# Cross attention of a decoder layer on one Trainium2 core: where VectorE's routing steps stand in a round

## The reference

```python
x = layernorm(x + linear_attention(x))                 # 16 heads of 8
lat, src = layer_norm(x), layer_norm(ctx)              # cross attention, 16 heads of 64
q = lat @ Wq;  k, v = split(concat([src, lat]) @ Wkv)  # 120 + 128 = 248 keys
x = layernorm(x + softmax(q k^T / 8) v @ Wout)
scores = softmax(x @ gate_w.T)                         # 8 experts, top 2
w = top2(scores) / (sum(top2) + 1e-20) * 2.5
x = layernorm(x + sum_e w_e * swiglu_e(x) + shared_swiglu(x))
```

## Time and profile before

| | |
|---|---|
| median of 3 runs | 2205.88 us (2205.7 to 2206.94) |
| the profiled execution's own time | 2202.96 us |
| its span | 2201.2 us |
| PE busy | 1994.3 us (91%) |
| DVE, ACT, POOL busy | 1551.4, 1258.4, 1322.8 us |
| start of the residual of the first and the last round (L922) | 396.2 and 1757.8 us |

### The profile page before, as it was taken

One profiled execution on the slowest core, in us unless ns is written; L12 is line 12 of the kernel. 1 busy time (PEld: TensorE's weight loads), 2 busy tenths in 40 slices (PEclk: granted clock), 3 DMA queues, 4 the chain that ended last, 5 costly groups with the idle time before them and its releaser, 6 DMA issues. The chain is left out here.

```text
span 2201.2 us, 47735 instructions
## 1 busy us (share of the span) xinstructions
PE 1994.3 (91%) x16155; PEld 1718.1 (78%) x16155; DVE 1551.4 (70%) x3978; ACT 1258.4 (57%) x3814; POOL 1322.8 (60%) x1485
## 2 busy tenths in 40 slices
PE   6799968999999999999999999999999839999971
PEld 3455547999999999999999999999999827888761
DVE  3799965777777777777777777777777725555654
ACT  3455545666666666666666666666666514444553
POOL 4688856566666666666666666666666533444564
PEclk9899979999999999999999999999999969999995
DMA  3411110000000000000000000000000022223334
GB/s 97 114 34 30 34 31 6 8 14 19 15 17 14 19 15 17 15 18 15 17 15 18 15 18 15 19 15 17 15 18 16 14 61 74 72 71 91 105 107 128
DMA packets 112148, 80.00 MB, mean 36 GB/s; under 512 B 11518, under 2 KB 105288, under 8 KB 111784
## 3 DMA queue, kind: packets, MB, share of 16 engines
q1 hardware_dynamic: 92420, 50.52, 8.3%
q0 software_dynamic: 8640, 17.97, 2.4%
q10 hardware_dynamic: 10852, 8.46, 1.4%
HBM read 44.34 MB, written 32.57 MB: 35 GB/s over the span
## 5 line engine op out<-in xcount | busy, mean ns | idle before, releaser
L745 POOL TENSOR_TENSOR x_prob<-x_prob,x_inv 128x496 f32<-128x496 f32 x514 | 521.7, 1015 | 501.8 <-DVE x_inv L916 347.9
L830 ACT ACTIVATE x_prob<-x_ps_S,x_nmax 128x248 f32<-128x248 f32 x1028 | 473.6, 468 | 250.4 <-DVE x_nmax L910 250.4
L910 DVE TENSOR_REDUCE x_nmax<-x_ps_S 128x2 f32<-128x496 f32 x515 | 344.4, 669 | 119.7 <-PE x_ps_S L519 119.7
L856 ACT COPY x_probT<-x_ps_T 124x512 f32<-124x512 f32 x512 | 300.6, 587 | 185.4 <-PE x_ps_T L1200 185.3
L517 PE MATMUL x_ps_S<-x_kT_lo,x_G_hi 128*128 128x248 f32 x1030 | 329.4, 320 | 0.0
L1200 PE MATMUL x_ps_T<-ident,x_prob 128*124 128x128 f32 x2048 | 318.6, 278 | 9.4 <-POOL x_prob L745 9.4
L1200 PEld LDWEIGHTS x_ps_T<-ident,x_prob 128*124 128x124 f32 x2048 | 235.6, 140 | 72.5 <-POOL x_prob L745 29.0
L519 PE MATMUL x_ps_S<-x_kT_hi,x_G_hi 128*128 128x248 f32 x1030 | 286.1, 278 | 0.0
L518 PE MATMUL x_ps_S<-x_kT_hi,x_G_lo 128*128 128x248 f32 x1030 | 285.0, 277 | 0.0
L1492 POOL DMA_INDIRECT sorted_results<-e_y,e_x_rows x142 | 145.8, 1026 | 198.8 <-DVE e_y L1621 189.3
L1142 PE MATMUL x_ps_O<-x_probT,x_V 124*64 124x128 f32 x4096 | 251.9, 276 | 0.5 <-ACT x_probT L856 0.5
(11 more groups left out here) (239 smaller groups left out, 4548.3 us busy)
## 6 DMA issues: line engine op xcount, KB each, us to landing
e_x_rows<-sorted_rows SPq DMA_DIRECT2D x142, 66.0 KB
x_nk<-latents SPq DMA_DIRECT2D x34, 124.0 KB
lin_x_rows<-in_x SPq DMA_DIRECT2D x32, 128.0 KB, 2.3
latents<-lin_nlat SPq DMA_DIRECT2D x32, 128.0 KB, 1.8
turned_rows<-w_rows SPq DMA_DIRECT2D x32, 128.0 KB, 1.7
e_all_xT<-turned_rows SPq DMA_DIRECT2D x32, 128.0 KB, 2.2
e_back<-sorted_results SPq DMA_DIRECT2D x16, 256.0 KB, 3.4
out_dram<-e_result SPq DMA_DIRECT2D x16, 256.0 KB
```

Of the source, the lines that this page charges most:

```text
L745: nc.gpsimd.tensor_tensor(prob[:, k], prob[:, k], inv[:, k].unsqueeze(2).broadcast_to([P, 2, K]), ALU.mult).then_inc(prob_ready, 1)
L830: nc.scalar.activation(prob[:, k, h, :], ps_S[:, n % BANKS, h * K:(h + 1) * K], ACT.Exp, bias=nmax[:, k, h:h + 1], accum_out=total[:, k, h ...
L856: nc.scalar.copy(probT[0:KT, s % (2 * GANG)], ps_T[0:KT, s % 2, :]).then_inc(probT_ready, 1)
L910: nc.vector.tensor_reduce(nmax[:, k, :], ps_S[:, n % BANKS, 0:2 * K].rearrange("p (h k) -> p h k", h=2), AX, ALU.max, negate=True).then_in ...
```

## The change

DVE's routing steps move in front of `maxima` in their slots. Making the weights (den, inv_den and two products) moves from slot 0, steps 16 to 19, to slot 8, where these are steps 22 to 25. The ranks and the rows keep slots 3 and 6. A step 15 is added, which copies the sum of the choices of both sequences to a third block of `picked`, so that the ranks and the growth of the base come from two products in place of four.

```diff
-    STEPS = 25
+    STEPS = 26
-        picked = room.sbuf("picked", [P, 3, EXPERTS], F32R)
+        picked = room.sbuf("picked", [P, 4, EXPERTS], F32R)
...
                     if s == 3 and later_round(r):
                         residual(r - 1)
+                    if r and s in ROUTE:
+                        route(r - 1, *ROUTE[s])
+                    if r > 1 and s in ROUTE_LATE:
+                        route(r - 2, *ROUTE_LATE[s])
                     maxima(unit + s + LEAD, (s + LEAD) % RINGS)
                     inverse(unit + s + 2, (s + 2) % RINGS)
                     if s == 7:
                         context_moments(r + 2, par)
-                    if r and s in ROUTE:
-                        route(r - 1, *ROUTE[s])
-                    if r > 1 and s in ROUTE_LATE:
-                        route(r - 2, *ROUTE_LATE[s])
...
-            ROUTE = {11: (0, 2), 13: (2, 6), 14: (6, 11), 15: (11, 16)}
-            ROUTE_LATE = {0: (16, 20), 3: (20, 22), 6: (22, STEPS)}
+            ROUTE = {11: (0, 2), 13: (2, 6), 14: (6, 11), 15: (11, 17)}
+            ROUTE_LATE = {3: (17, 19), 6: (19, 22), 8: (22, STEPS)}
...
                     elif k == 14:
-                        done = v.tensor_tensor(picked[:, 1:3], chosen[:, 0], chosen[:, 1], ALU.add)
+                        done = v.tensor_tensor(picked[:, 1:4:2], chosen[:, 0], chosen[:, 1], ALU.add)
                     elif k == 15:
+                        done = v.tensor_tensor(picked[:, 2], picked[:, 1].bitcast(F32), picked[:, 3].bitcast(F32), ALU.add)
+                    elif k == 16:
                         done = v.tensor_tensor(two, top, second, ALU.add)
...
+                    elif k == 22:
+                        done = v.scalar_tensor_tensor(den, z, 1e-20, two, ALU.mult, ALU.add)
+                    elif k == 23:
+                        done = v.reciprocal(inv_den, den)
+                    else:
+                        if k == 24:
+                            dve.wait_ge(staged_ready, n * 2 + 2)
+                        done = v.scalar_tensor_tensor(staged[:, par, k - 24, :, D + 1], (top, second)[k - 24], ROUTE_SCALE,
+                                                      inv_den, ALU.mult, ALU.mult)
...
             def ranks(n):
-                pe.wait_ge(routed, n * STEPS + 15)
+                pe.wait_ge(routed, n * STEPS + 16)
                 pe.wait_ge(outT_ready, min((n + 2) * GANGS, ROUNDS * GANGS))
-                flat = picked[:].rearrange("p k e -> p (k e)")
                 at = 3 * S
-                nc.tensor.matmul(ps_O[:, at:at + 2 * EXPERTS], before[:], flat[:, EXPERTS:3 * EXPERTS], start=True, stop=False)
-                nc.tensor.matmul(ps_O[:, at:at + 2 * EXPERTS], ones[:], flat[:, 0:2 * EXPERTS], start=False, stop=True)
-                at += 2 * EXPERTS
-                nc.tensor.matmul(ps_O[:, at:at + EXPERTS], ones[:], flat[:, EXPERTS:2 * EXPERTS], start=True, stop=False)
-                nc.tensor.matmul(ps_O[:, at:at + EXPERTS], ones[:], flat[:, 2 * EXPERTS:3 * EXPERTS], start=False, stop=True
-                                 ).then_inc(rank_psum, 1)
+                nc.tensor.matmul(ps_O[:, at:at + 3 * EXPERTS], ones[:], picked[:, 0:3].rearrange("p k e -> p (k e)"),
+                                 start=True, stop=False)
+                nc.tensor.matmul(ps_O[:, at:at + 2 * EXPERTS].rearrange("p (u e) -> p u e", u=2), before[:],
+                                 picked[:, 1:4:2], start=False, stop=True).then_inc(rank_psum, 1)
```

More of the change, by code:

```diff
@@ L977, in route @@
                         dve.wait_ge(score_ready, n + 1)
-                    elif k == 20:
+                    elif k == 17:
                         dve.wait_ge(rank_psum, n + 1)
@@ L1007, in route @@
                     elif k == 14:
-                        done = v.tensor_tensor(picked[:, 1:3], chosen[:, 0], chosen[:, 1], ALU.add)
+                        done = v.tensor_tensor(picked[:, 1:4:2], chosen[:, 0], chosen[:, 1], ALU.add)
                     elif k == 15:
+                        done = v.tensor_tensor(picked[:, 2], picked[:, 1].bitcast(F32), picked[:, 3].bitcast(F32), ALU.add)
+                    elif k == 16:
                         done = v.tensor_tensor(two, top, second, ALU.add)
-                    elif k == 16:
-                        done = v.scalar_tensor_tensor(den, z, 1e-20, two, ALU.mult, ALU.add)
@@ L1013, in route @@
                     elif k == 17:
[L1014 to L1020, removed]
                         done = v.tensor_tensor(place[:], rank, base.unsqueeze(1).broadcast_to([P, 2, EXPERTS]),
@@ L1022, in route @@
                                                ALU.add)
-                    elif k == 21:
+                    elif k == 18:
                         done = v.tensor_tensor(base, base, grown, ALU.add)
-                    elif k == 22:
+                    elif k == 19:
                         done = v.tensor_tensor(taken[:], chosen[:], place[:].unsqueeze(1).broadcast_to([P, 2, 2, EXPERTS]),
                                                ALU.mult)
-                    elif k == 23:
+                    elif k == 20:
@@ L1029, in route @@
                         done = v.tensor_reduce(goes[:], taken[:], AX, ALU.add)
-                    else:
+                    elif k == 21:
                         wait(dve, slots.scattered[par], n // 2 * 64)
                         done = v.tensor_copy(slot[:, par], goes[:])
+                    elif k == 22:
[7 more added lines that the diff above has]
+                                                      inv_den, ALU.mult, ALU.mult)
@@ L1065, in _ @@
             residual(ROUNDS - 1)
-            route(ROUNDS - 2, 16, STEPS)
+            route(ROUNDS - 2, 17, STEPS)
             route(ROUNDS - 1, 0, STEPS)
@@ L1235, in body @@
                         if s == 4 and r > 1:
-                            pe.wait_ge(routed, (r - 2) * STEPS + 22)
+                            pe.wait_ge(routed, (r - 2) * STEPS + 19)
                         gang_output(r * GANGS + s // GANG - 1)
@@ L1259, in _ @@
             ranks(ROUNDS - 2)
-            pe.wait_ge(routed, (ROUNDS - 2) * STEPS + 22)
+            pe.wait_ge(routed, (ROUNDS - 2) * STEPS + 19)
             turn_rows(ROUNDS - 1)
```

## The result

| | before | after |
|---|---|---|
| median of 4 runs | 2205.79 us (2205.43 to 2206.94) | 2176.46 us (2175.79 to 2179.48) |
| the profiled execution: own time, span | 2202.96, 2201.2 us | 2175.79, 2174.1 us |
| from the first residual (L922) to the last | 1361.6 us | 1333.9 us |
| one round in the steady part | 44.06 us | 43.11 us |

The changed kernel takes 0.9869 of the time of before, with a 95% interval of 0.9852 to 0.9886: 29 us faster. The forecast was 2186 us, with a range of 2173 to 2204. The span is 27.1 us shorter, and the stretch from the first to the last residual is 27.7 shorter; what lies outside it comes to 0.6 the other way. So the gain is one of the rounds: 0.95 us in each where 0.70 was forecast.

A forecast was written before the change was run, and what follows sets the result against it. TensorE was taken as the bound, busy 43.40 of 44.08 us a round. The terms -0.67 - 0.22 - 0.16 - 0.11 + 0.46 gave -0.70 a round, x 29 = -20.3 us: 2186 us, range 2173 to 2204.

The forecast's parts named there:

- Slot 2: TensorE's `output` would no longer wait for DVE's `V_copy`, the weights' four steps having left slot 0: -0.67 us a round.
- Ranks: Two fewer TensorE products at 0.11 us: -0.22 us a round, with the added DVE step in slot 15 hidden.
- "uncovered" price: Cost of the ranks' added DVE step in slot 15 if TensorE's work did not hide it: 0.2 us.
- Slot 0's transposes: An earlier inverse of unit 16 in slot 14 would let POOL's multiply and these transposes start earlier: -0.16 us a round.
- Step 10: DVE step in slot 14, taken as not held by POOL's `normalise_context`: -0.16 us a round; if held, 0.
- `x_ps_G` in slot 0: `G_lo` of slot 15 comes right behind the inverse, so this product's late start goes: -0.11 us a round.
- Slot 9: TensorE's `x_ps_V` would start later, behind POOL's delayed `keys_lo`, from the steps in slots 6 to 8: +0.46 us a round.
- Step 24: DVE weights step in slot 8, taken as held by POOL's `keys_hi`: +0.46 us a round at `x_ps_V`; if free, +0.30.
- the cast: DVE's cast of the rows in slot 6, arriving in the middle of POOL's `normalise`, was taken as free, at 0.17 us.
- rivals 1 and 2: POOL's tensor_scalar holds DVE's steps, in its middle and later part (2200 us, chance 0.24) or from its first moment (2213, 0.10).
- rival 3: Nothing changes, as slot 2's wait passes to another of TensorE's waits: 2205 us, chance 0.07.
- rival 2: POOL's tensor_scalar holds DVE's steps from its first moment: +0.24 us a round, 2213 us, chance 0.10.

The follow-up runs named there:

- e1: The changed kernel with the routing steps put back behind maxima and inverse, weights still in slot 8, ranks two products: 2193.23 us, ratio 0.9956.
- e6: e4 with all routing steps put back behind maxima and inverse, weights in slot 10: 2179.68 us, ratio 0.9896.
- e3: e2 with the routing steps in front of the maxima, weights staying in slot 0: 2157.22 us, ratio 0.9795.
- e2: The kernel before with only the ranks as two products and the added step: 2203.16 us, ratio 1.0004.
- e4: The changed kernel with the weights' steps 22 to 25 in slot 10 instead of slot 8, still before the maxima: 2157.20 us, ratio 0.9795.
- e8: The changed kernel with POOL's multiply of a unit as two tensor_scalars in place of one tensor_tensor: 2282.44 us (one run).

## Why the prediction was right, point by point

- **Slot 2, -0.67 forecast, -0.77 measured.** The wait went as said. The step missed that TensorE, once it has waited, also runs the first of what follows more slowly: 3.59 for the 32 products of `output` behind the wait, 3.49 without. I had counted this for `x_ps_G` in slot 0, where the profile shows a product of 0.39 for 0.28, and not here, where the group of 32 hides it. The reason given, that the weights leave slot 0, was sufficient but not needed: e1 and e6 have them out and the steps behind, and have no such wait; e3 keeps them in slot 0 and loses the wait by the place of the steps.
- **Ranks, -0.22, measured -0.23** (0.22 from the first of them to the transposes, 0.45 in the earlier trace rows). The added step was hidden, as said. e2 shows the condition: where slot 2 waits for DVE, the step costs 0.20, the "uncovered" price of the prediction, and the two products' gain is gone with it.
- **Slot 0's transposes, -0.16, measured -0.13** in the rounds shown (0.33 late, now 0.20), -0.15 as the median of the steady rounds. Step 10 was free, as chosen.
- **`x_ps_G` in slot 0, -0.11, measured -0.17:** a wait of 0.07 in front of the slow product, which I had left out.
- **Slot 9, +0.46, measured +0.39** (0.11 late before, 0.50 now). Step 24 was held by `keys_hi`, 0.31 for 0.16; no row of before had a step against a cast on POOL, and the row taken instead, the multiply, led right. The place, the cause and the sign are confirmed by e4, where slot 9's whole loss goes with the four steps.
- **The sum.** -0.77 - 0.23 - 0.13 - 0.17 + 0.39 = -0.91 of the measured -0.95 a round, where -0.70 was forecast. The terms were mis-sized by the restarts (0.10) and by 0.06 and 0.07 in two waits. The median came 29 us down where 20 were forecast.
- **The rivals.** The tensor_scalar held neither the cast in its middle nor step 10, so rivals 1 and 2 don't occur. Nothing took the place of slot 2's wait (rival 3). The Trainium skill, page SBUF — State Buffer, section Who interferes with whom, makes no exception for a tensor_scalar on GpSimd. The trace of after does not agree in two places: the cast took 0.17 at 0.32 inside one, and the step with two SBUF inputs 0.17 at 0.52 inside another. In e8 it agrees for the first half only: steps that meet the start of a tensor_scalar of 0.91 are held, but to 0.47 to 0.50 behind its start and not to its end. Step 8 of after, 0.08 behind the start of `normalise_context`, took 0.20 for 0.17, where rival 2 had it held to the end. For a tensor_tensor the trace agrees (1.03 in e6's longest case).
- **What the prediction did not see.** It costed the change as it stood, and could not say which part pays. The experiments do: the steps in front of the maxima bring 1.54 us a round where the weights stay in slot 0 (e2 to e3), and 0.65 where they are in slot 10 (e6 to e4). Moving the weights is worth something only in the old order: 0.41 a round to slot 8 (e2 to e1), 0.89 to slot 10 (e2 to e6). In the new order the move to slot 8 costs 0.58 a round (e3 to after), about 17 us, and the one to slot 10 brings nothing (e3 and e4 are the same). After is the kernel e3 with that cost added.

Why does the front pay? In slot 13 DVE idles 0.57 in front of its maxima for TensorE's scores, in slot 10 of e6 0.66, and POOL is between two multiplies. Steps there cost DVE time that it has. Behind the inverse they stand where POOL has just been released: e1's 2.02, e6's 1.03 for one step. How much each does can be read from e4 and e6, which differ in nothing else. Between slot 13's transposes and DVE's `V_copy` of slot 0 both have the same 15 steps, and that copy starts 9.41 behind the transposes in e6 and 7.32 in e4 (medians of the steady rounds), 2.09 earlier. The three held steps of e6 (0.82, 1.03 and 0.82) and the two of e4 (0.42 and 0.58) account for 1.5 of it, the idle 0.57 of slot 13 for nearly all of the rest. So the hold by POOL is the larger part of DVE's gain; how much of TensorE's 0.65 each part would bring alone stays open, since no run has the one without the other.

## What to carry to other kernels

When several engines share a tight loop, list every place at which the bottleneck engine stands still in one period, with its length and the slower product behind it, and cost an edit by what it does to each. Cost its side effects in the same way: one small step of 0.2 on DVE was free in after, and cost 0.20 a round in e2, where TensorE waited for the end of DVE's chain, as much as the two saved products brought. Filler work on DVE belongs in front of the instruction that DVE idles for and not behind the one that starts POOL, and it should keep clear of slots whose POOL work ends in something that the bottleneck waits for (slot 8 to 9 here). And when a change has several parts, try each with and without the others: here the new order brought most of the gain, the two products paid only where their step was hidden, and the move, worth 0.41 in the old order, took 0.58 back in the new one.

## What the runs showed of the hardware

- A wait of TensorE costs more than its length: the first of the products behind it takes 0.47 for 0.39 (`x_ps_V`) or 0.38 for 0.28 (`x_ps_G`), and a group of 32 takes 0.10 more.
- POOL's tensor_tensor of 496 elements (1.01), its subtraction (1.25) and its cast (0.59) held DVE's steps with two SBUF inputs until they ended, and the multiply held the cast too (0.78). Reductions were not held: L998 has at most 0.171 us inside a multiply, in all runs. Its tensor_scalars did not hold to their end: one of 248 elements (0.91) held such steps until 0.47 to 0.50 behind its start (e8), and in one of 128 elements (0.80) a step 0.08 behind the start took 0.20 for 0.17.
- Two tensor_scalars of 248 elements cost POOL 1.8 us where one tensor_tensor of 496 costs 1.01.
